# The averages of the first linear attention formed transposed, in four column groups of the array

## The reference, cut to what matters

```python
qp = jax.nn.elu(jnp.einsum('bhcsd,hdf->bhcsf', q, proj)) + 1.0
kp = jax.nn.elu(jnp.einsum('bhcsd,hdf->bhcsf', k, proj)) + 1.0
kv = jnp.einsum('bhcsf,bhcsd->bhcfd', kp, v)
num = jnp.einsum('bhcsf,bhcfd->bhcsd', qp, kv)
ksum = kp.sum(axis=3)
z = 1.0 / (jnp.einsum('bhcsf,bhcf->bhcs', qp, ksum) + 1e-08)
out = num * z[..., None]
...
return out @ w_out.T + b_out
```

## Time and profile before

| what | value |
|---|---|
| runs | 1266.7, 1274.31, 1274.86 us; median 1274.31 |
| profiled execution | 1260.86 us, its span 1259.1 us |
| busy in the span | PE 1128.0, PEld 714.2, DVE 902.0, ACT 697.0, POOL 510.6 us |
| mean granted clock of TensorE | 0.93 |

### The profile page before, as it was taken

One profiled execution on the slowest core, in us unless ns is written; L12 is line 12 of the kernel. 1 busy time (PEld: TensorE's weight loads), 2 busy tenths in 40 slices (PEclk: granted clock), 3 DMA queues, 4 the chain that ended last, 5 costly groups with the idle time before them and its releaser, 6 DMA issues.

```text
span 1259.1 us, 15646 instructions
## 1 busy us (share of the span) xinstructions
PE 1128.0 (90%) x5494; PEld 714.2 (57%) x5494; DVE 902.0 (72%) x2074; ACT 697.0 (55%) x1167; POOL 510.6 (41%) x482
## 2 busy tenths in 40 slices
PE   7999999899999999999999776899998978639977
PEld 6765544355445574655544323597776746318967
DVE  4856437556658857779799998685688799956554
...
PEclk8999999999999879999999875898999989659999
...
GB/s 266 194 1 1 1 1 0 1 1 1 1 17 1 1 1 1 18 1 1 1 1 1 0 0 17 149 87 180 126 82 101 109 16 97 16 127 217 236 254 118
DMA packets 39838, 76.86 MB, mean 61 GB/s; under 512 B 3281, under 2 KB 29009, under 8 KB 39249
## 3 DMA queue, kind: packets, MB, share of 16 engines
...
...
## 4 chain that ended last, share of the span: by engine, by line
PE 55%; DVE 13%; ACT 11%; POOL 10%; issue 6%; DMA 5%; POOLq 0%; SPq 0%; DVEq 0%; ACTq 0%
PE ps L894 7%; PE ps L2161 5%; PE ps L1469 4%; PE ps L2169 3%; PE ps L1278 2%; DVE own L2027 2%; PE ps L1287 2%; PE ps L668 2%; DMA g_f<-w,slot 2%; PE ps L856 2%; POOL sx L2414 2%; POOL own L2051 2%; PE ps L654 2%; POOL own L2446 1%; PE ps L1589 1%
## 5 line engine op out<-in xcount | busy, mean ns | idle before, releaser
L894 PE MATMUL ps<-own,g_f 128*128 128x512 f32 x320 | 146.1, 597 | 1.1 <-DVE own L1103 1.1
L1221 POOL TENSOR_TENSOR own<-own 128x512 f32<-128x512 f32 x32 | 43.4, 1355 | 162.4 <-PE ps L894 92.1
L894 PEld LDWEIGHTS ps<-own,g_f 128*128 128x128 f32 x320 | 59.1, 191 | 66.8 <-issue 58.4
L2027 DVE TENSOR_TENSOR_SCAN own<-own,carry 128x512 f32<-128x512 f32 x48 | 77.2, 1608 | 20.4 <-POOL own L2051 17.1
L2051 POOL TENSOR_TENSOR own<-own 128x512 f32<-128x512 f32 x32 | 51.9, 1622 | 77.6 <-ACT own L1977 77.6
L1931 PE MATMUL ps<-own,g_c 128*128 128x512 f32 x64 | 45.2, 795 | 40.7 <-POOL own L2057 40.5
L2238 ACT ACTIVATE own<-ps 128x512 f32<-128x512 f32 x60 | 35.7, 596 | 79.6 <-PE ps L2161 79.0
L1968 ACT ACTIVATE own<-own,Acol 128x512 f32<-128x512 f32 x64 | 45.2, 714 | 56.4 <-PE ps L1931 56.2
L2352 DVE TENSOR_TENSOR own<-ps,own 128x512 f32<-128x512 f32 x60 | 41.1, 684 | 47.1 <-PE ps L2161 40.2
L526 ACT ACTIVATE own<-xs,sm 128x128 f32<-128x128 f32 x128 | 52.5, 482 | 31.1 <-POOL sm L518 31.0
L1887 POOL TENSOR_TENSOR own<-own 128x512 f32<-128x512 f32 x32 | 43.6, 1365 | 55.4 <-DVE own L1861 51.7
...
## 6 DMA issues: line engine op xcount, KB each, us to landing
...
```

Of the source, the lines that this page charges most:

```text
L894: x = e.matmul(s.bank["V%d%d%d" % (it, k, cc)][:, :], ew2[:, m, 128 * cc:128 * cc + 128], gm, start=False, stop=m == 3)
L1221: e.tensor_tensor(R.gm[m % 2], R.g[m], R.mask[k][m], ALU.mult).then_inc(*s.pool.up("m%d%d%d" % (it, k, m)))
L2027: e.tensor_tensor_scan(H, A, H, init, ALU.mult, ALU.add).then_inc(*s.dve.up("H%d" % n))
```

## The change: four column groups, and transposes back

In `mix` the operands change places. The 32 columns of `vext` that begin at a head's 17 are now the stationary operand, the masked scores of one tile (128x128) move past them, and tile i writes PSUM partitions 32i to 32i+31, in the four column groups of the array. The 15 columns behind a head's 17 are those of the next head, and are not used; `vext` gets 32 more columns, set to zero, so that they exist for the last head. Heads 0 to 3 fill one bank (`nd0`), heads 4 to 7 the other (`nd1`). ACT copies each bank to SBUF (`averaged`), four transposes for each bring tokens back to partitions (`turned`, banks `ot0` and `ot1`), and DVE works on two groups of four heads. `ORDER` is another string throughout (39 lines instead of 38).

```diff
-        vext = [sb(f"vext{i}", [128, 4, 8, 17]) for i in range(2)]
+        vflat = [sb(f"vext{i}", [128, 576]) for i in range(2)]
+        vext = [v[:, 0:544].rearrange("p (t h n) -> p t h n", t=4, h=8) for v in vflat]
...
+            for v in vflat:
+                e.memset(v[:, 544:576], 0.0)
...
             def mix(hd):
                 q.wait_ge(*s.dve("s%d" % hd))
-                b = T[c][8 + hd % 2]
-                p = banks.take(s, q, "nd1", (s.dve, "o1")) if hd == 7 else s.bank["nd0"]
+                b, p = T[c][8 + hd % 2], s.bank["nd%d" % (hd // 4)]
                 for i in range(4):
-                    o = 17 * i if hd == 7 else 119 * i + 17 * hd
-                    m = e.matmul(p[:, o:o + 17], tl(b, i), vx[:, i, hd, :], start=True, stop=True)
+                    at = 17 * (8 * i + hd)
+                    m = e.matmul(p[32 * i:32 * i + 32, 128 * (hd % 4):128 * (hd % 4) + 128], vflat[c % 2][:, at:at + 32], tl(b, i), start=True, stop=True)
                 m.then_inc(*s.pe.up("n%d" % hd))
+
+            def turned(j):
+                p = banks.take(s, q, "ot%d" % j, (s.dve, "o%d" % j))
+                q.wait_ge(*s.act("nd%d" % j))
+                for k in range(4):
+                    m = e.transpose(tl(p, k), tl(T[c][1 + j], k), V["ident"])
+                m.then_inc(*s.pe.up("ot%d" % j))
...
-                if hd == 3:
+                if hd in (3, 7):
                     yield
-                    banks.hold(s, q, "nd0", (s.dve, "o0"))
+                    banks.hold(s, q, "nd%d" % (hd // 7), (s.act, "nd%d" % (hd // 7)))
...
-            banks.back(s, "nd0")
+                if hd in (6, 10):
+                    banks.back(s, "nd%d" % (hd // 10))
+                if hd >= 9:
+                    yield
+                    turned(hd - 9)
...
+            def averaged(j):
+                q.wait_ge(*s.pe("n%d" % (4 * j + 3)))
+                e.activation(T[c][1 + j], s.bank["nd%d" % j][:, :], ACT.Copy).then_inc(*s.act.up("nd%d" % j))
...
-            for j, (h0, h1) in enumerate(((0, 7), (7, 8))):
+            for j, (h0, h1) in enumerate(((0, 4), (4, 8))):
                 n = h1 - h0
                 z = sm[c][:, 500 + 28 * j:500 + 28 * j + 4 * n].rearrange("p (t n) -> p t n", t=4)
-                v4 = s.bank["nd%d" % j][:, 0:68 * n].rearrange("p (t n k) -> p t n k", t=4, n=n)
+                q.wait_ge(*s.pe("ot%d" % j))
+                v4 = s.bank["ot%d" % j][:, :].rearrange("p (n t k) -> p t n k", t=4, n=n)
```

More of the change, by code:

```diff
@@ L38 @@
[L38 to L61, removed]
@@ new lines @@
+    "cmmbmcgamcfccfmaammfhbbbkgkgghaacfcchhhackfbmbbmpccchddlkhkdcnkcllnpchpbpcplfdmlbnllhagdrddnfnbbnbgmigigbkpbbplnnmblltal"
+    "aaallflmabffgaakakfffakfkkbbbgrdfraanrrgbfaghkkkklbdklgaanfbbdffngbafnaannfeboaafodfaikpdldfkdiakakgtdkdkafqiakkddfkiiki"
+    "caadflddhakaallanqqknnoaaqqgpakaaaaafpffbakgaapffkdkakkndpdndnddinindnddfdidfidfddniindnfdkdkdkddinnnidndkdiknddkinkidid"
+    "nddnaiaiadfaffdaafidfadkdikdkaaakpniasfnnaaqfqfnalsfsksbbbsiagbfbggfbbllgblggdlbgliaagafbbagllbplfllaafbfaaaagggggakfglb"
@@ new lines @@
+    "pbkaalllkaklklaapabbkabkfalgbfkbqblgaflfakfkkkaapkkkapbbblfbbblbfbfgfgblgfbbqkkblkbbqbkbbgkgkbgkkbqlagagbllflfalafqaafab"
+    "kkagkgfagkcrkccrmgklcpplhlhhpcphlccflclclhhpmhambbfmgbmgmfbghbbgagcckhcmmmammkcfchahhchcchcbffclchaclhmhcrlchmcqbbbhmlhm"
+    "bmmgmbbglgmbmgmmbgagfcccccfcfmfkffkccrfkfkfaamffkafbbffcgfahrhafaffkcckkfccchkkfkkfcmfkhaaraamfmaffcckfmffkkaafkfckfhkkf"
+    "kaaamfrafkfakkfakfkffaaakfkbffbkakqbbahkgaagbbhbbghagkbkhlfmmaqmbbkmkklblllaqlbbbflbalkgbbkggmgkbmppmglplpcqcflclbbllhlh"
@@ new lines @@
+    "qacfcchhbhcggamgamamgkkrcccmfkkfkkcgkfkkakkhkahamlalfhcckkkkkflafkakfckfklahlhkaalkallkkakkkckkkahakkkkkkkbbgkgabkkbgkkk"
+    "bbkgkcccblalaklgckkkccrbbckkklcccklhuhlhuqkqcmhqkppcchkqgrmmpmpcqfmmmpamccccrcchhhhcmfhaafrmakakakaakkakafkcckpkfpckfpmk"
+    "amahmafmfaphmbhrkghbpkfgbkphaglbmalgmgamffbbpmgmagpkgbgakfggapkgfalfgplbgllpggblgmbgmbgmgalgbggkgbbcbglllgclfgpclllhahbh"
+    "kgkbkkcgkbbglgllccggklbhclgbbgmllgbggmblgcgbmlgbllbhlgclggbgmblgdssdddmglllfbkbbkiaiimldfrnrbianngrlddkrhbkdkiirdlilinpp"
@@ new lines @@
+    "cddlnhlphpnbpcigndfmnbnnnclmlahcfldhaqiqiiakkiqdqkidddfgkdkakkdkkhckkiinbsnangnfbnfnnbllbglglbllblgbllblllgnlblglllgblkg"
+    "allbgklkbblkkbkkflblllllclhllbhhblmhlhhlblmhhlllhmmbhllmblllllallcclfllhlclhlclhlchhlvvmhqdhhmmcqmihdmqdqdniccmmhdaingnc"
+    "dddlddhqhibnmdggbbsblblblddlllbbndllbisiabgkikddqdgddklqfpdnilabgsikddnqlpbagngaqkndfqnkaslbfbakilailgafaqpakiakabkfapfa"
+    "kkaikbnaanfpnfagkbkfqangkbqflpaaalgaqklafafabknbkbkgpncfhkqgkalqchchpbmhmmhhamchhnmddhmmcghdkqcikbimkichplpdlclphplcmcfl"
@@ new lines @@
+    "ddmmhdplinaccfnhahnmhhamshahnmmdddhkfmcfkicmcgclalcimbangchkbmmcldmfmlmfclfddkhqqkffkcfqkqgqmdmmdrirkkiibrkrgaahakaaaakb"
+    "ikibllfddflpchlbkiclcmmfcmmfmfamghmfhhcplllmlmkmcmpmhllkhckhmfmcmmmcmmhckhcmmkbccgmgllcllclllgcmmmmmambmmmambkamgaammmbk"
+    "mbfmblbflfbqlblbglbgkqbgbglblbkqlbblgblglbqlgaalfbbgpbfllbgqlagapkbbaqkkblblfalbfbfkfbpkclgpkgafcgqlklabkqamammmabmmmafm"
+    "aladffkdfdkdislfdidddpilpkiaqkqkdfnqffqkgkddsnnqnabnfdfgpnnpnkaaasbkiakialfalabffkafdikbpgbfgpkbigaklakgdglfadlggldgddlf"
@@ L72 @@
+    "nnndnnnx"
 )
@@ L1372, in l1a_scalar @@
                         project(n)
+                if hd == 7:
+                    yield
+                    averaged(0)
                 yield
                 yield from maps(hd)
+            yield
+            averaged(1)
             yield
```

32 lines of the change are left out of this document (18 added, 14 removed).

## The result

| | before | after |
|---|---|---|
| median of the runs | 1271.2 us (4 runs, 1266.7 to 1274.86) | 1288.47 us (4 runs, 1287.26 to 1291.57) |
| profiled execution, its span | 1260.86, 1259.1 us | 1287.26, 1285.1 us |
| mean granted clock | 0.93 | 0.927 |

The ratio is 1.016, with a 95% interval of 1.011 to 1.021 (the two medians alone divide to 1.014): the changed kernel is slower, where the forecast had it 0.8% faster.

What follows compares the result with a forecast made beforehand. PE was taken to bound the linear-attention stretches, with DVE full at 700 to 780 us. 1274.3 less 6.3 us passed on from PE and 4 of the clock, order 0, gave 1264.0 us; range 1245 to 1287 us.

Steps and rivals of the forecast that it cites:

- the order: The new ORDER string throughout, strand 2's heads moved back: counted at 0 us.
- The bound of 8 us: Allowance for the new ORDER string: 8 us on either side, for the range.
- Rival 3: Column groups don't overlap, or the order loses some 20 us despite full overlap: 1286 us, chance 0.15 together.
- The mix: Each of 32 mixes on PE: 0.55 us instead of 0.90, saving 11.2 us in all.
- The sum on PE: Mixes save 11.2 us on PE, added transposes cost 3.5: net 7.7 us less.
- Rivals 2 and 3: Mixes on PE: only pairs overlap, 0.77 us, 1272 us, chance 0.18; or none overlap, 1.20 us, 1286 us, within 0.15.
- list of signs: What the changed profile would show: mix start to next product about 0.5 us against 0.81; over 0.79 means no overlap.
- The rule of the Trainium skill: Weight loads overlap a matmul only in another row group; by it the mixes lose 7.7 us in all.
- What passes on: PE savings reaching the end: 5.8 us from strands 0 to 2, 0.5 from strand 3, together 6.3 us.
- The clock: Two slow stretches of PE, at 440.2 and 532.4 us, cost 10.2 us together; four tenths, 4 us, taken as gained.
- ACT and the hand-overs: Two bank copies for each strand on ACT, 4.8 us in all, expected to be hidden by ACT's idle time.
- The end of a strand: Copy, transposes and hand-overs behind the last mix: net 0.2 to 0.4 us longer, counted for strand 3 only.

Runs made afterwards that it cites:

- e2: Old code of the mixes in the changed kernel's order, against the kernel before: 1277.02 us, ratio 1.018.
- e13: The changed kernel again, unaltered, on the chip of e12, against the kernel before: 1268.57 us, ratio 1.014.
- e1: Changed mixes, copies and transposes in the old order, against the kernel before: 1253.81 us, ratio 0.998.
- e12: e1 with the new order only between the ends of strand 1's and strand 2's L1A, against the kernel before: 1264.78 us, ratio 1.010.
- e6: Changed mixes, new order up to the end of strand 1's L1A (473 us), old behind it, against the kernel before: 1277.99 us, ratio 1.007.
- e9: e1 with each mix's products issued twice, against the kernel before: 1251.15 us, ratio 0.996.
- e8: e1 again, unchanged, on another chip, against the kernel before: 1252.92 us, ratio 0.998.
- e11: e1 with the second group's transposes two PE steps behind the last mix instead of three, against the kernel before: 1250.92 us, ratio 0.995.

## Why the prediction was wrong

**The failed step is the order.** "I count 0, with 8 us on either side for the range": it costs 1.8% by e2 against the kernel before, 22 to 23 us, and 1.6% (1.014 by 0.998) by e13 against e1, some 20 us. The prediction even held that moving strand 2's heads towards a stretch where PE waits "may save a few us in the DVE stretch". It read the right rows, 470 to 560 with PE full and 700 to 780 with DVE full, and drew the wrong end from them: what must be fed ahead of 700 us is DVE, the engine that is full there. Nor is it true that the heads go to a stretch where PE waits. The mixes of the moved heads stand at 578 to 603 us in the changed kernel, and in the kernel before both engines were nearly full there (columns as in the earlier trace rows):

```profile
575.00:605.00 30.00, 28.35 (x142) 18.19 (x142) 29.65 (x43) 15.52 (x25) 15.92 (x11) 1.00 0.00 1
```

By e12 this stretch of the order costs 1.2% alone, with 13.2 us less of DVE's work done ahead of 700 us; what the order loses ahead of 473 us (e6) stays open in its cause. The bound of 8 us had no row behind it. Rival 3 named the case ("the same end is reached with full overlap if the order loses some 20 us") and gave 1286 us, which is within 3 us of the result, but put it into 0.15 with a rival that was worked out and is wrong.

**The mix was forecast rightly, in its parts too.** 0.55 us were forecast and 0.55 measured: 0.09 ahead of the mix, 0.36 from its start to the next product, of which 0.21 are the passes (e9), and 0.10 for the weights behind it. The sum on PE holds with it: 32 x 0.35 = 11.2 us saved and 8 x 0.43 = 3.4 spent, net 7.8 where 7.7 was said. Rivals 2 and 3 in its worked-out form are excluded: 0.55 is far from 0.77 and 0.79. (The prediction's list of signs holds the 0.79 against the step from a mix's start to the next product. It is a bound on the whole excursion, since 0.90 is one.) That all 32 pay in full is not quite so: two of them stand ahead of a product in 32 columns and take 0.24 us instead of 0.36. The rule of the Trainium skill that spoke against the change ("TensorE: Matmul & The Clock Gate", Part 3, what overlaps and what doesn't: a load overlaps only with products in other row groups) would have given 1.4 us (an estimate); the trace disagrees with it here, since four groups that share all their rows finish eight loads and passes in 0.36 us, and the loads of the second round begin 0.03 us behind the first pass of the first (302.157 and 302.130 in the records). That page's 2.38 times for three column groups would have given 0.36 us for the passes alone (an estimate); e9 measured 0.21.

**"What passes on" was too large.** 6.3 us of PE and 4 of the clock should have reached the end. In the old order, where the mixes can be judged, 3 us did (e1, e8; 7 at most by the interval). PE's work did shrink: busy time from strand 0's heads to strand 2's in the kernel before run again,

```profile
235.00:400.00 165.00, 164.48 (x574) 80.46 (x573) 105.73 (x235) 106.53 (x162) 38.84 (x35) 1.00 0.01 4
400.00:470.00 70.00, 66.67 (x318) 44.42 (x317) 50.76 (x105) 46.25 (x79) 21.16 (x22) 0.80 0.00 1
470.00:560.00 90.00, 86.46 (x400) 49.12 (x400) 68.62 (x188) 55.16 (x96) 22.92 (x24) 0.98 0.02 7
```

and in e1:

```profile
235.00:400.00 165.00, 162.03 (x573) 75.11 (x573) 103.16 (x231) 106.24 (x163) 37.43 (x35) 1.00 0.01 4
400.00:470.00 70.00, 65.24 (x359) 39.65 (x358) 53.64 (x114) 51.58 (x90) 24.20 (x26) 0.88 0.00 1
470.00:560.00 90.00, 82.91 (x401) 42.70 (x400) 70.41 (x191) 54.67 (x95) 23.32 (x21) 1.00 0.02 7
```

Of the 325 us PE is idle for 7.4 in the first and 14.8 in the second, and strand 3's L0F ends 3.0 us sooner (757.8 against 760.8). e8, the same kernel as e1, is idle for 12.0 us there, and its L0F of strand 3 ends 1.7 us sooner (759.1). The 24 mixes less their transposes give PE some 5.8 us back in these stretches (24 x 0.35 - 6 x 0.43), and 4.6 to 7.4 us more of idle time stand against them. So, as far as three profiles tell, most of what the mixes gave up became waiting: a PE busy for 99% of a stretch hid waits that stood just behind it, and the scores, features and products of the heads still go round over ACT and DVE. "There a microsecond taken from PE should move everything behind it" holds for a part of them at most. The lead then moves on unchanged through DVE's full stretch, as was said: e1 is 3.1 us ahead of the kernel before run again at the end of strand 2's L1A, and 3.0 at the end of strand 3's L0F. It is 9.2 at the end of strand 3's L3A, but the two ran on different chips.

**The clock.** 4 us were forecast, from two slow stretches of one profile. The second, at 532 us, is missing from the only other profile of the same kernel (from 500 to 551 us its clock is 1.00, and was 0.93), so it was no fixed property of the code. Over many executions the mean granted clock rises with the changed mixes in the old order from 0.933 to 0.937 on both chips (standard errors 0.001), worth 3 to 4 us by the line above. That agrees with the forecast; then nothing is left of the 6.3 us of PE, or only what the interval allows. How the 3 us divide is open. In the new order the clock falls (0.926 against 0.936 in e13), worth 8 to 9 us of its 18 by the same line; whether the waits pull the clock down or the clock makes the waits, no run here separates.

**ACT and the hand-overs.** The copies take 0.59 us, and PE waits for them at L1297 for 0.4 us at most (e11). Elsewhere it waits for a bank that a copy frees: 0.5 us at L942, 0.4 at L890 and 1.4 at L2193 in e8, 2.3 in all, and none in the changed kernel's own order. The prediction had costed 4.8 at most and counted 0. The end of a strand was counted for strand 3 alone, since "for strands 0 to 2 other work fills it". In e8 that cover was thin: DVE waited 5 us more at the averages than before, and 4.1 us in all at strand 0, where 0.6 stood before, since three PE steps stand between head 7's mix and the second transposes. In the changed kernel's own order these waits are 4.4 us in all, less than the 6.4 of the kernel before. Three positions of the transposes give 0.994 to 0.998.
